# A recurrent kernel in halves: the order of tiles and products between the halves, and an announced loop branch

## The reference

```python
def step(h, xs):
    xzt, xrt, xht = xs
    z = sigmoid(xzt + h @ U_z + vz)
    r = sigmoid(xrt + h @ U_r + vr)
    hh = tanh(xht + r * h @ U + vh)
    h_new = (1.0 - z) * h + z * hh
    return h_new, h_new
```

## Time and profile before

| | us |
|---|---|
| median of 3 runs | 7111.71 |
| lowest and highest run | 7102.33, 7116.66 |
| the profiled execution | 7111.03 |
| its span, first to last instruction | 7109.2 |
| TensorE busy, matmuls | 6224.6 (88%) |
| VectorE busy | 5234.9 (74%) |
| ScalarE busy | 3359.5 (47%) |
| DMA, mean | 19 GB/s |
| TensorE's clock granted, mean | 0.971 |

### The profile page before, as it was taken

One profiled execution on the slowest core, in us unless ns is written; L12 is line 12 of the kernel. 1 busy time (PEld: TensorE's weight loads), 2 busy tenths in 40 slices (PEclk: granted clock), 3 DMA queues, 4 the chain that ended last, 5 costly groups with the idle time before them and its releaser, 6 DMA issues.

```text
span 7109.2 us, 488208 instructions
## 1 busy us (share of the span) xinstructions
PE 6224.6 (88%) x200232; PEld 5779.7 (81%) x200232; DVE 5234.9 (74%) x43503; ACT 3359.5 (47%) x22603; POOL 3.5 (0%) x13
## 2 busy tenths in 40 slices
PE   7888888888888888888888888888888888888888
PEld 7888888888888888888888888888888888888887
DVE  6777777777777777777777777777777777777777
ACT  3444444444444444444444444444444444444444
POOL 0000000000000000000000000000000000000000
PEclk8999999999999999999999999999999999999999
DMA  2000000000000000000000000000000000000000
GB/s 81 19 17 16 17 19 17 19 15 19 17 19 17 15 18 19 17 19 15 18 17 19 17 18 15 19 17 19 17 16 17 19 17 19 15 19 17 18 17 16
DMA packets 80595, 134.55 MB, mean 19 GB/s; under 512 B 12336, under 2 KB 18480, under 8 KB 80304
## 3 DMA queue, kind: packets, MB, share of 16 engines
q1 hardware_dynamic: 80304, 129.81, 5.3%
HBM read 20.46 MB, written 8.65 MB: 4 GB/s over the span
## 4 chain that ended last, share of the span: by engine, by line
PE 68%; DVE 26%; issue 5%; ACT 0%; SPq 0%; DMA 0%; ACTq 0%; DVEq 0%
PE pair_r L252 27%; PE ps_z L252 23%; PE pair_h L252 17%; DVE pair_h L481 8%; DVE h_part L528 4%; DVE h_part L518 4%; DVE h_part L537 4%; DVE keep L519 2%; DVE h_part L523 2%; DVE zn L532 2%; PE ps_p L224 0%; PE ps_z L212 0%; DMA u_raw<-in_L_cond_U 0%; DVE rh_part L490 0%; DVE ps_z L481 0%
## 5 line engine op out<-in xcount | busy, mean ns | idle before, releaser
L252 PEld LDWEIGHTS pair_r<-h_part,u_part 128*128 128x128 f16 x65536 | 1783.8, 96 | 1146.9 <-DVE h_part L537 1027.8
L252 PE MATMUL pair_r<-h_part,u_part 128*128 128x32 f16 x65536 | 1985.4, 177 | 801.9 <-DVE h_part L537 686.2
L252 PE MATMUL pair_h<-rh_part,u_part 128*128 128x32 f16 x65536 | 2120.3, 177 | 9.7 <-DVE rh_part L499 8.3
L252 PE MATMUL ps_z<-h_part,u_part 128*128 128x32 f16 x65536 | 1971.2, 177 | 45.4 <-issue 45.4
L252 PEld LDWEIGHTS pair_h<-rh_part,u_part 128*128 128x128 f16 x65536 | 1907.2, 96 | 104.4 <-DVE rh_part L499 11.6
L252 PEld LDWEIGHTS ps_z<-h_part,u_part 128*128 128x128 f16 x65536 | 1802.2, 96 | 48.0 <-issue 48.0
L481 DVE TENSOR_REDUCE pair_r<-pair_r 128x4 f32<-128x20 f32 x4096 | 742.4, 186 | 744.8 <-PE pair_r L252 723.4
L345 ACT ACTIVATE pair_r<-pair_r 128x4 f32<-128x4 f32 x4096 | 640.6, 158 | 1360.8 <-DVE pair_r L481 1291.5
L481 DVE TENSOR_REDUCE pair_h<-pair_h 128x4 f32<-128x12 f32 x4096 | 717.7, 175 | 697.7 <-PE pair_h L252 697.7
L345 ACT ACTIVATE th_z<-ps_z 128x8 f32<-128x8 f32 x2048 | 362.6, 177 | 1132.8 <-DVE ps_z L481 1132.8
L345 ACT ACTIVATE pair_h<-pair_h 128x4 f32<-128x4 f32 x4096 | 647.0, 158 | 393.4 <-DVE pair_h L481 393.0
(11 more groups left out here) (70 smaller groups left out, 3299.5 us busy)
## 6 DMA issues: line engine op xcount, KB each, us to landing
w_stage<-w_in SPq DMA_DIRECT2D x384, 256.0 KB, 2.3
x_tok<-in_x SPq DMA_DIRECT2D x68, 128.0 KB, 2.6
out_dram<-o_tok SPq DMA_DIRECT2D x66, 128.0 KB, 2.4
mlp_w<-in_L_cond_W SPq DMA_DIRECT2D x2, 1024.0 KB, 6.8
u_raw<-in_L_cond_U_r SPq DMA_DIRECT2D x1, 1024.0 KB, 5.6
u_raw<-in_L_cond_U_z SPq DMA_DIRECT2D x1, 1024.0 KB, 7.7
u_raw<-in_L_cond_U SPq DMA_DIRECT2D x1, 1024.0 KB, 10.4
w_in<-in_L_cond_W_r SPq DMA_DIRECT2D x4, 256.0 KB, 9.8
```

The source lines that it names most:

```text
L252: last = nc.tensor.matmul(bank[:, SLOT * m:SLOT * m + WIDE].rearrange("p (r n) -> p r n", n=n), u_part[:, g, part, k, gm * P:(gm + 1) * P] ...
```

## The change

Three edits.

**TensorE's order of tiles.** `staggered` replaces the loops of r and of h. In the product of a gate, first the input's half 0 for both tiles of bank 0 and for the first tile of bank 1 (12 matmuls), then the wait for half 1, then half 1 for bank 0 (8 matmuls, bank 0 is done), then the second tile of bank 1 with half 0 (4), then bank 1 with half 1 (8). For r the wait for half 1 stood after 16 matmuls, for h after 8. z is as it was.

**VectorE's order.** high, full and low of r*h are done for half 0 and then for half 1; before they were interleaved. The second sum of h stands ahead of `new_high(0)` rather than behind it.

```diff
+            def staggered(banks, g, parts, src, name, t1):
+                def product(mh, m, kh):
+                    for k in range(kh * HC, (kh + 1) * HC):
+                        last = tile_product(banks[mh], m, g, mh * HC + m, k, parts, k == 0 and m == 0)
+                    return last
+                pe.wait_ge(s[src + "0"], t1)
+                for m in range(HC):
+                    product(0, m, 0)
+                product(1, 0, 0)
+                pe.wait_ge(s[src + "1"], t1)
+                for m in range(HC):
+                    last = product(0, m, 1)
+                last.then_inc(s[name + "0_mm"], 1)
+                for m in range(1, HC):
+                    product(1, m, 0)
+                for m in range(HC):
+                    last = product(1, m, 1)
+                last.then_inc(s[name + "1_mm"], 1)
...
-                    for kh in range(2):
-                        pe.wait_ge(s[f"hs{kh}"], t1)
-                        for mh in range(2):
...
+                    staggered(ps_r, R, h_part, "hs", "r", t1)
...
-                    for mh in range(2):
-                        for kh in range(2):
-                            if mh == 0:
-                                pe.wait_ge(s[f"rh{kh}"], t1)
...
+                    staggered(ps_h, H, rh_part, "rh", "h", t1)
...
-            with pe.Fori(0, NB) as n:
+            with nc.Fori(0, NB, engines=[mybir.EngineType.PE], hint_back_edge=True) as n:
...
-                gated_high(0)
-                gated_full(0)
-                gated_high(1)
-                gated_low(0)
-                gated_full(1)
-                gated_low(1)
+                for hf in range(2):
+                    gated_high(hf)
+                    gated_full(hf)
+                    gated_low(hf)
...
-                new_high(0)
                 dve.wait_ge(s["h1_mm"], t1)
                 total(ps_h[1], H, HC, "h1_sum")
+                new_high(0)
                 new_full(0)
```

## The result

The changed kernel takes **6812.28 us** (6811.76 to 6815.90, 4 runs) against 7112.88 us before: ratio 0.9581, 95% interval 0.9564 to 0.9597, so 301 us or 4.2% less.

What follows compares the result with a forecast made beforehand. The prediction saw one serial loop of waits between TensorE (68%) and VectorE (26%), plus code-load stalls at the outer back edge. 7111 - 115 (orders) - 90 (hint) = 6906, given as 6905 us, range 6850 to 7000.

Steps and rivals of the forecast that it cites:

- D: In each step, time from the first r matmul to the arrival of hs1 at TensorE; predicted 0.35 us, before 0.40.
- the walk: Tracing one step through the new TensorE and VectorE orders with measured hops: step falls from 3.35 to 3.28 us.
- rival 2: In each step, the time to hs1's arrival stays at 0.40, 0.03 us less gained: 6965 us; chance 0.13.
- rival 5: Nothing moves: TensorE's stall in r and h eats the order's gain, the hint is void: 7110 us; chance 0.02.
- 52 x 0.06 + 12 x 0.04, 115 us: Orders' gain per outer turn, 52 common steps and 12 delayed by store_projection: 3.60 us, times 32 is 115 us.
- I keep these 45 us as they are: At the outer back edge, TensorE's second stall, inside the z product (45.4 us in 31 times), stays despite the hint.
- the 90 us for the target's own stall: At the outer back edge, before the r product: announcing the branch target ahead saves 90 us of code-load waiting.
- Rival 3: The stall inside z goes too, the sequencer asking for the next piece while awaiting hs0: 6860 us; chance 0.07.
- rival 4: Slower: the announced piece is loaded in each of 12 inner-loop passes, pushing out a needed one: 8025 us; chance 0.04.
- The fifth step: Last step of an inner iteration, where store_projection holds VectorE and delays r's first sum: gain 0.04 us, not 0.06.

Runs made afterwards that it cites:

- no_sum_first: The changed kernel with h's second sum back behind new_high(0), all else changed: 7100 us, ratio 1.0003.
- hint_only: The kernel before with only the hint, the announced closing branch of TensorE's outer loop, both orders as before: 6967 us, ratio 0.9803.
- store_early: The changed kernel with the two address products of VectorE's projection store computed ahead and kept in registers: 6799 us, ratio 0.9578.
- both_addresses: The kernel of store_early with ScalarE's ring address for the next pass's seeds also computed ahead and kept in a register: 6785 us, ratio 0.9542.

## Where the prediction was right and where it failed

**The sign and both mechanisms of the orders: right.** D moved as the walk said, from 0.40 to 0.33 (0.35 predicted); the sum of half 1 sits in the wait for the tanh; new_full(0) follows at once. Rivals 2 and 5 did not happen, though what lies behind rival 2 is real: with the sum in its old place D stays at 0.39, and the whole gain of the orders goes and 133 us more (`no_sum_first` 7100, `hint_only` 6967). I had asked the right question and answered it with too small a number, 60 us: I had kept the sum in front in that rival, which is the very thing that moves D.

**The size of the orders' gain: too small.** The term "52 x 0.06 + 12 x 0.04, 115 us" measured 154 to 158 us. The common step fell by 0.086 us (16.76/5 was the mean over a pass; the four common steps of a pass are 3.344, and they are 3.258 now). The walk ended at 3.28 where the trace has 3.26, because it put 0.08 between any two instructions of VectorE, and behind the short products it is 0.07 (2844.19 to 2844.26; 2844.53 follows 2844.45 by 0.08). Most of the difference enters through D, 0.33 and not 0.35, so that r's first sum starts at 0.73 and not at 0.75. And of the 0.06 to 0.07 that the walk gave I took the smaller. 0.026 times 1664 common steps is 43 us.

**"I keep these 45 us as they are": wrong**, and this is the step whose mechanism failed. It did not put the time out of the range alone: 6905 less 45 is 6860, less 43 is 6862, both within it, and it took the two together. I held that the hint names the branch target and not the piece behind it, so that the second stall must stay. The runs show that the second piece needn't be fetched at all: with the hint all eight are held (8 loads in the run, no stall in z, 142 us for the hint). That makes the 90 us for the target's own stall luck in their cause: they came, but not because the target was loaded earlier in each turn; it was not loaded at all. Rival 3 gave 6860 for the loss of this stall, at a chance of 0.07, and by another cause (a fetch hidden behind a wait), which did not happen. I had the number in hand that decides it: nine pieces a turn, a body of 1785 instructions in pieces of 256, which is seven or eight. The ninth had no instruction of the loop in it. I noted it under rival 4 as harmless and never asked why it was loaded, nor what it pushed out.

**The rest.** 43 and 45 of the missing 93 us (6905 less 6812) are these two terms. The remaining 5 I put down to the edges, where before the first steps of a turn ran in stretches of the lower clock behind the stalls; the row of the kernel before shows 0.80 granted in the first 17 us of a turn, that of the kernel after 1.00 in such a stretch:

```profile
509.20:526.00 16.80, 13.64 (x435) 12.80 (x435) 11.53 (x88) 7.37 (x47) 0.00 (x0) 0.80 0.17 43
```

```profile
286.00:310.00 24.00, 21.16 (x712) 19.78 (x709) 18.21 (x153) 12.47 (x80) 0.00 (x0) 1.00 0.11 33
```

(Columns: stretch, its length, busy time and number of instructions of PE, PEld, DVE, ACT, POOL, the granted clock, DMA share, GB/s.) What share of those 5 us the clock has was not measured apart.

**The fifth step**: predicted gain 0.04, measured 0.045 (3.386 to 3.341). Right in size, but the delay was put down to VectorE's store alone; with VectorE's address work gone half of it is still there (3.302 against 3.261), and goes with ScalarE's (3.261), as `store_early` and `both_addresses` show.

## What to carry to other kernels

Count the pieces of code that an outer loop loads per turn and hold them against the pieces that its body spans: if one more is loaded than the body needs and the body itself fits, as here with eight, the gain to be had is every load of the turn, not only the branch target, and it was to be had either by the hint or by the loop's place in memory. In a loop where two engines hand halves to each other, walk the order through until the state that one step hands to the next repeats itself (here the distance between the two halves' arrivals), since a good part of an edit's effect may be on that. Orders of two engines that are made for each other must be judged together: TensorE's alone and VectorE's alone each made the kernel slower by 1.3 to 3.5%.

## What the runs showed of the hardware

TensorE held 8 pieces of 16 KB of instructions over 32 turns and reloaded everything at 9: 8 or 9 loads in the run against 288 to 320. The inner loop, 960 matmuls and weight loads and some more instructions, was loaded at most once a turn, in its first pass, and in none of the eleven others, in any kernel. Without the hint one piece more than the body spans is loaded a turn, 9 against 8 and 10 against 9, and by its time it is the one behind the loop's end; with the hint it is not. Two address products taken out ahead of VectorE's store brought the store forward by 0.18 us (0.60 to 0.42 of the step) and shortened the step by 0.04; taking the modulo out ahead of ScalarE's seed brought the seed forward by 0.07 (2.26 to 2.19) and shortened the step by another 0.04.
